# A four-layer graph network: four adjacency blocks built early, relation counts made turned

## What is computed

```
L0: key = x W_w + b; e = leaky_relu(s_dst[dst] + s_src[src]); alpha = softmax over dst
    x = LN(x + segment_sum(alpha * key[src], dst))
L1: x = LN(x + relu((x + segment_sum(x[src], dst)) @ W))
L2: messages silu(x[src] @ W + b) * edge weight, mean over dst, two-layer update, LN
L3: agg = segment_sum((x[src] + rel_emb[type]) @ W_msg.T + b_msg, dst) / degree; LN
```

## Time and profile before

| | |
|---|---|
| median of three runs | 1089.4 us (1089.07 to 1090.24) |
| the profiled execution | 1089.84 us, span 1088.0 us |
| PE busy | 1002.6 us, 92% of the span |
| PEld busy | 874.7 us, 80% |
| DVE busy | 861.1 us, 79% |
| ACT busy | 691.3 us, 64% |
| POOL busy | 218.2 us, 20% |

### The profile page before, as it was taken

The page is one execution under the profiler, slowest core; times in us unless marked ns, Lnnn a source line. Parts: engine busy times, 40 slices in busy tenths (PEclk is TensorE's granted clock), DMA queues, the critical chain, the costliest instruction groups (busy, mean ns, idle before and its releaser), DMA issues.

```text
span 1088.0 us, 27899 instructions
## 1 busy us (share of the span) xinstructions
PE 1002.6 (92%) x10463; PEld 874.7 (80%) x10463; DVE 861.1 (79%) x1934; ACT 691.3 (64%) x1489; POOL 218.2 (20%) x260
## 2 busy tenths in 40 slices
PE   3798979699999999995999999779999999989997
PEld 3343557599999999995788889669999999976775
DVE  6875999988998989987766677788787888766754
ACT  3467765454555555456888888577677776776554
POOL 4501340000000000000000000126666666610000
PEclk9899999899999999997999999889999999999998
DMA  6000020366767677752866564235444445334232
GB/s 159 1 2 1 4 68 3 121 207 225 238 215 225 222 238 227 204 175 72 292 195 193 172 201 141 82 104 140 138 136 129 131 131 139 109 112 124 69 99 82
DMA packets 86925, 150.38 MB, mean 138 GB/s; under 512 B 14524, under 2 KB 58375, under 8 KB 86557
## 3 DMA queue, kind: packets, MB, share of 16 engines
q1 hardware_dynamic: 65609, 116.01, 35.9%
q10 hardware_dynamic: 16122, 22.16, 5.7%
q0 software_dynamic: 5056, 10.36, 3.9%
HBM read 112.56 MB, written 35.94 MB: 136 GB/s over the span
## 4 chain that ended last, share of the span: by engine, by line
PE 81%; DVE 10%; ACT 4%; issue 3%; DMA 2%; POOL 0%; POOLq 0%; DVEq 0%; SPq 0%; ACTq 0%
PE PS L2500 14%; PE PS L2705 14%; PE PS L2488 11%; PE PS L2688 8%; PE PS L2611 7%; PE PS L2791 6%; PE PS L2581 3%; PE PS L2588 3%; PE PS L2326 2%; PE PS L2339 2%; DVE ring L1659 2%; DVE vo L1663 2%; PE PS L2403 2%; ACT X L1227 1%; PE PS L2357 1%
## 5 line engine op out<-in xcount | busy, mean ns | idle before, releaser
L1151 ACT CAST vo<-XT 128x768 f32<-128x768 bf16 (+1 forms) x218 | 180.3, 827 | 163.7 <-PE PS L2705 64.2
L984 POOL DMA_INDIRECT XT<-tab,ring x158 | 159.9, 1012 | 113.5 <-PE PS L2705 60.2
L2500 PE MATMUL PS<-vo 128*128 128x133 f32 x1300 | 175.9, 284 | 1.2 <-ACT vo L1151 1.2
L2500 PEld LDWEIGHTS PS<-vo 128*128 128x128 f32 x1300 | 157.2, 191 | 1.4 <-issue 1.4
L2488 PE MATMUL PS<-kp,ring 128*128 128x132 bf16 x1950 | 146.7, 221 | 3.2 <-DVE ring L1631 1.7
L2705 PE MATMUL PS<-vo 128*128 128x128 f32 x984 | 132.8, 279 | 0.0
L2488 PEld LDWEIGHTS PS<-kp,ring 128*128 128x128 bf16 x1950 | 125.6, 97 | 5.4 <-DVE ring L1631 1.8
L1641 DVE TENSOR_TENSOR XT<-iotab,XT 128x768 bf16<-128x768 bf16 (+1 forms) x218 | 120.0, 551 | 3.2 <-DMA hots_d<-XT 1.5
L2705 PEld LDWEIGHTS PS<-vo 128*128 128x128 f32 x984 | 118.9, 191 | 3.0 <-issue 2.4
L2490 PE MATMUL PS<-SDP,ring 128*128 128x12 bf16 x650 | 110.2, 170 | 0.0
L1286 ACT CAST adjf_r<-PS 128x512 fp32r<-128x512 f32 (+1 forms) x175 | 92.4, 550 | 25.4 <-PE PS L2581 23.6
(11 more groups left out here) (350 smaller groups left out, 2008.6 us busy)
## 6 DMA issues: line engine op xcount, KB each, us to landing
ring<-rows_d SPq DMA_DIRECT2D x146, 416.0 KB, 5.8
hots_d<-XT ACTq DMA_DIRECT2D x108, 192.0 KB, 4.7
big<-hots_d SPq DMA_DIRECT2D x10, 640.0 KB, 5.3
XT<-hots_d SPq DMA_DIRECT2D x10, 640.0 KB, 4.8
adj_d<-ring SPq DMA_DIRECT2D x20, 320.0 KB, 2.4
big<-hots_d SPq DMA_DIRECT2D x8, 480.0 KB, 4.4
adj_d<-ring SPq DMA_DIRECT2D x15, 240.0 KB, 2.1
ring<-adj_d SPq DMA_DIRECT2D x11, 320.0 KB, 3.0
```

The source lines that it names most:

```text
L984: G.indirect_dma_start(far_rows[:, f % FBUF, :], None, tab[2], bass.IndirectOffsetOnAxis(ap=far_row[:, t:t + 1], axis=0)).then_inc(far_in[ ...
L1151: C.copy(ohd[:, k % 3, 0:n, :], ohb[:, k % 3, 0:n, :]).then_inc(hots_wide, 1)
L2500: T.matmul(bank(6 + b % 2)[:, 0:VW], ohd[:, k % 3, i, :], vals[:, k % 3, i, :], start=j == 0, stop=j == JN - 1).then_inc(scattered, 1)
```

## The change

- `set_hots(0, NB)` and `set_hots(0, 0)` to `set_hots(0, 3)` move from the normalisation and layer one into layer zero's batches 103 to 106 on DVE. The copy of `SLc` that they need moves on ACT from behind layer zero into batch 101.
- SP loads the extras and chunks 0 and 1 as soon as the one-hots of the first four blocks are stored (18 batches). The wait for all stores moves ahead of chunks 2 and 3. These still stand behind `rc_cp` and the two DMAs of the reciprocal counts.
- PE builds steps 0 to 3 right after the last sum is copied, then transposes the reciprocal counts, then applies 0 and 1, builds 4 and 5, and so on.
- ACT widens steps 0 to 3 before the roots. Its byte copies of steps 0 and 2 stand behind `round_rows` 0 and 1 and behind `round_rows` 2. The last four rows (`ACT2`) are scaled one by one in steps 6 to 9, and `round_rows` 3, 4, 5 and 6 move to steps 5, 10, 12 and 14. DVE's `XL` 3 to 6 move to steps 6, 11, 13 and 15.
- The relation product has the 64 type columns as its stationary operand and moves the 128 columns of the destination one-hots. The result is turned already. `crelT`, its copy and `rel_turned` go; `rel_rows` reads bank 5 or 6 at step 2 of the next group. The product of zeros moves twice the columns and writes 64 partitions.
- The dense products wait for the last byte copy on ACT, for the last `sums_out1` from bank 3 on, and for `rel_rows` from bank 5 on.

```
+    EARLY_HOTS = HT * (NU - 1) // BT - 3
+    AHEAD = 4
+    LATE_ROWS = XBUF + 2
+    def rounded_at(i):
+        return XBUF + 1 if i < HBANK else LATE_ROWS + len(ACT2) + 2 * (i - HBANK)
 SP:
-                sp.wait_ge(hots_out[r], hots_stored(r))
+                sp.wait_ge(hots_out[r], 16 * len(range(r, (len(even(0)) * JN - 1) // BT + 1, 3)))
             extra_load(0); hots_load(0); hots_load(1)
...
                 if n == 0:
                     sp.wait_ge(hots_wide, NBATCH)
+                    for r in range(3):
+                        sp.wait_ge(hots_out[r], hots_stored(r))
                     hots_load(2)
 ACT:
+                if k == EARLY_HOTS - 2:
+                    C.copy(SLc[:, 1, :, :], SLc[:, 0, :, :]).then_inc(pairs_ready, 1)
...
+            for s in range(XBUF):
+                block_wide(s)
             for h in range(2):
                 deviations(1, h)
             act.wait_ge(scale_ready, 1)
             scaled_rows(X, range(0, QNB))
             for i in range(QBANK):
                 round_rows(1, i)
+            block_byte(0)
+            block_byte(1)
             scaled_rows(X, range(QNB, HNB - 4))
             for i in range(QBANK, HBANK - 1):
                 round_rows(1, i)
-            act.wait_ge(scale_ready, 2)
-            scaled_rows(X, ACT2)
+            block_byte(2)
+            block_byte(3)
             act.wait_ge(rc_tr, 1)
...
                     if s >= XBUF:
+                        block_wide(s)
+                        block_byte(s)
+                    if q == 0 and b == LATE_ROWS:
+                        act.wait_ge(scale_ready, 2)
+                    if q == 0 and 0 <= b - LATE_ROWS < len(ACT2):
+                        scaled_rows(X, [ACT2[b - LATE_ROWS]])
+                    for i in range(HBANK - 1, BANKS):
+                        if q == 0 and b == rounded_at(i):
+                            round_rows(1, i)
+                    if q and b == 2:
                         rel_rows(q - 1)
-                act.wait_ge(rel_mm, (q + 1) * NB)
-                C.copy(crelT[:, q % 2, 0:w // 2], bank(5 + q % 2)[:, 0:w // 2]).then_inc(crelT_cp, 1)
 DVE:
+                if k == EARLY_HOTS:
+                    dve.wait_ge(pairs_ready, 3)
+                    set_hots(0, NB, ohx[:, 0, :])
+                if 0 <= k - EARLY_HOTS < AHEAD:
+                    set_hots(0, k - EARLY_HOTS, ohs[:, k - EARLY_HOTS, :])
...
-                            if b == min(1 + i, NB - 1):
+                            if b == (1 + i if i < HBANK - 1 else rounded_at(i) + 1):
                                 dve.wait_ge(xp_top, i + 1)
 PE:
+                if s == 0:
+                    pe.wait_ge(vals_ready, NBATCH)
+                    pe.wait_ge(sums_cp, NB)
...
-                    o = T.matmul(bank(5 + q % 2)[:, d * NREL:(d + 1) * NREL], d1, r1, start=False, stop=False, skip_group_check=True)
+                    o = T.matmul(bank(5 + q % 2)[0:NREL, d * P:(d + 1) * P], r1, d1, start=False, stop=False, skip_group_check=True)
...
-            build(0)
-            build(1)
+            for s in range(XBUF):
+                build(s)
+            pe.wait_ge(cnt_ready, 1)
+            T.transpose(bank(4)[0:NB, 0:P], rc[:, :], ident[:, :]).then_inc(rc_tr, 1)
             for s in range(0, NS, 2):
                 for n in (s + 2, s + 3):
-                    if n < NS:
+                    if XBUF <= n < NS:
                         build(n)
                 for n in (s, s + 1):
                     if n < NS:
                         apply1(n)
-                        if n >= NB and n % NB == 7:
-                            rel_turned(n // NB - 1)
-            rel_turned(BANKS - 1)
...
             def sums1_wait(i):
                 pe.wait_ge(ag_ready, (even_need(i) if i < 3 else BANKS))
-                if i == 3:
+                if i == 5:
                     pe.wait_ge(crel_cp, BANKS)
-                if i >= 5:
-                    pe.wait_ge(crelT_cp, BANKS)
                 if i == 0:
+                    act_copied(pe, NS - 1)
                     pe.wait_ge(rc_cp, 1)
```

More of the change, by code:

```diff
@@ L1255, in round_rows, with block_wide, block_byte @@
                 C.copy(XH[:, nodes(i), :], X[:, nodes(i), :]).then_inc(xp_top, 1)
+            def block_wide(s):
+                w = even_width(s // NB)
+                act.wait_ge(adj_mm, s + 1)
+                if s >= XBUF:
+                    act.wait_ge(applied, s - XBUF + 1)
+                    dve_copied(act, s - XBUF)
+                C.copy(adjf[:, s % XBUF, 0:w], adj_bank(s)[:, 0:w]).then_inc(adjf_cp, 1)
+            def block_byte(s):
+                if not by_dve(s):
+                    adj_free(act, s)
+                    C.copy(adj_slot(s), adj_bank(s)[:, 0:even_width(s // NB)]).then_inc(adj_act, 1)
+            for s in range(XBUF):
+                block_wide(s)
             for h in range(2):
@@ L1651, in _, with set_hots @@
             FIRST = [h for h in units_at(0) if HT * h < 2 * BT]
+            def set_hots(q, j, buf):
+                V.tensor_tensor(buf.rearrange("p (k n b) -> p k n b", k=3, b=4), IN1[:, :, :].rearrange("p (k n) b -> p k n b", k=3),
+                                SLc[:, :, j, 4 * q:4 * q + 4].unsqueeze(2).to_broadcast([P, 3, NREL, 4]), ALU.is_equal).then_inc(ohs_ready, 1)
             dve.wait_ge(pool_consts, 8)
@@ L1923, in normalise @@
                     variance(1)
-                    set_hots(0, NB, ohx[:, 0, :])
                     scale(0)
@@ L1947, in split @@
                 low(BANKS - 1)
[L1949 to L1953, removed]
             normalise(1, X)
@@ L1985, in _ @@
                         sums_out1(q - 1)
-            for s in range(BANKS * NB - 4, BANKS * NB):
+            for s in range(BANKS * NB - AHEAD, BANKS * NB):
                 adj_copy(s)
@@ L2558, in build @@
                     if q >= 2:
-                        pe.wait_ge(crelT_cp, q - 1)
-                    T.matmul(bank(5 + q % 2)[:, 0:even_width(q) // 2], zeros[0:1, 0:P], zeros[0:1, 0:even_width(q) // 2],
+                        pe.wait_ge(crel_cp, q - 1)
+                    T.matmul(bank(5 + q % 2)[0:NREL, 0:even_width(q)], zeros[0:1, 0:NREL], zeros[0:1, 0:even_width(q)],
                              start=True, stop=False, skip_group_check=True)
                 pe.wait_ge(ohs_ready, q * JN + b + 2)
-                if s == 3:
-                    pe.wait_ge(rc_cp, 1)
+                if s == 0:
+                    pe.wait_ge(vals_ready, NBATCH)
+                    pe.wait_ge(sums_cp, NB)
                 if s >= 4:
@@ L2587, in build @@
                     _, d1, r1 = hots(*usual, d)
-                    o = T.matmul(bank(5 + q % 2)[:, d * NREL:(d + 1) * NREL], d1, r1, start=False, stop=False, skip_group_check=True)
+                    o = T.matmul(bank(5 + q % 2)[0:NREL, d * P:(d + 1) * P], r1, d1, start=False, stop=False, skip_group_check=True)
                     if b == 0:
                         _, d1, r1 = hots(*extra, d)
-                        o = T.matmul(bank(5 + q % 2)[:, d * NREL:(d + 1) * NREL], d1, r1, start=False, stop=False, skip_group_check=True)
+                        o = T.matmul(bank(5 + q % 2)[0:NREL, d * P:(d + 1) * P], r1, d1, start=False, stop=False, skip_group_check=True)
                 o.then_inc(rel_mm, 1)
-            def rel_turned(q):
-                pe.wait_ge(crelT_cp, q + 1)
-                pe.wait_ge(ag_ready, q + 1)
-                for d in range(len(even(q))):
-                    o = T.transpose(bank(3 + q % 2)[0:NREL, d * P:(d + 1) * P], crelT[:, q % 2, d * NREL:(d + 1) * NREL], ident[:, :])
-                o.then_inc(crel_tr, 1)
             def apply1(s):
@@ L2604, in apply1 @@
                 if b == 0 and q >= 2:
-                    pe.wait_ge(crel_cp, q - 1)
+                    pe.wait_ge(ag_ready, q - 1)
+                if b == 0 and q == 1:
+                    pe.wait_ge(rc_cp, 1)
                 if q == 0:
```

33 lines of the change are left out of this document (10 added, 23 removed).

## The result

The changed kernel takes 1133.24 us (median of 4 runs, 1132.64 to 1135.62), the kernel before 1089.82 us beside it (4 runs). The ratio is 1.0407, with a 95% interval of 1.0394 to 1.042: slower by 4%. The profiled execution took 1135.62 us with a span of 1133.8, against 1089.84 and 1088.0 before.

What follows compares the result with a forecast made beforehand. PE was taken as the limit, with 81% of the chain. +2.2 - 2.4 + 0.6 + 0 - 1.25 gave -0.85 us at the relu, taken as -0.7: median 1088.7 us, range 1085.5 to 1093.0.

Steps and rivals of the forecast that it cites:

- Part 6: Turned relation product, 650 on PE: bounds 0 to +4.5 us, -1.5 not excluded, taken as zero; narrow load held hidden.
- Rival 2: Turned product slower than before in each of 171 later builds: up to +4.5 us, 1093.2; chance 0.16.
- Rival 3: Load of 64 columns stands bare before each of 630 turned products, at least 0.05 us each: +31 us, 1120; chance 0.05.
- part 1: Early one-hots on DVE, loads on SP and copy on ACT in layer zero's late batches: cost zero.
- parts 1 and 2: Early one-hots, loads and copy cost zero; copy of the reciprocal counts (`rc_cp`) on ACT comes 1.0 us earlier.
- rival 4: PE starts late (501.4), table load delays the roots, `rc_cp` only 0.2 earlier: sum 0, 1089.5; chance 0.10.
- part 3: Blocks before chunk 2: build(10) starts at 523.9, PE idle 2 us; of about 3 us lead 1.0 is kept.
- Rings: ACT's round, DVE's `XL` and one-hots, PE's block at steps 10, 12, 14: 3.25, 3.25, 2.55 us; loss 3.2 us.
- part 4: Added wait three times in steps 10 to 16: loses 3.2 us, step 16 at 533.0, 2.2 us later than before.
- parts 5 and 7: Transposes gone from PE -2.4 us, larger product of zeros +0.6; dense products earlier at layer one's end -1.25.

Runs made afterwards that it cites:

- e5: Changed kernel with two neighbouring steps' adjacency products first, then their relation products, so half as many changes of width: 1112.97 us, ratio 1.0212.
- e1: Changed kernel with 128 loaded columns in the relation product (64 sources and 64 types) instead of 64: 1085.92 us, ratio 0.997.
- e7: Kernel before with only the relation product turned, at 128 loaded columns, in the old order of blocks: 1083.3 us, ratio 0.9946.
- e12: Changed kernel with 72 loaded columns in the relation product instead of 64: 1093.41 us, ratio 1.0032.
- e4: Changed kernel with 96 loaded columns in the relation product instead of 64: 1106.41 us, ratio 1.0145.
- e2: Changed kernel with the relation product, its copy and transposes as before, leaving the new order alone: 1092.24 us, ratio 1.0023.
- e9: e1 with DVE's subtractions of groups 3 to 6 two steps later, behind the one-hots PE waits for: 1084.03 us, ratio 0.9949.
- e8: Changed kernel with the 64 loaded columns' results in partitions 64 to 127 instead of 0 to 63: 1134.24 us, ratio 1.0403.

## Why the prediction was wrong

**Part 6 is the step that failed**, and it alone. It took the turned product at zero, with 0 to +4.5 us as bounds, "by the nearest row, the adjacency product beside it". That row has the moved side right and the loaded side wrong: it loads 128 columns, where the turned product loads 64. The one row with 64 loaded columns was the fp32 transpose, whose four follow each other and the apply without a gap, and from it I concluded that a narrow load is hidden. In those fp32 rows it is. In bf16, with the same 128x64 in the trace's rows, each change into it or out of it costs 0.135 us (e5), 4 changes to a pair. That makes 0.60 us for each pair against full width, and 0.57 against before. Fed with that, the prediction's own sum comes out: the 159 steps from step 16 on are some 80 pairs, by 0.57 45.6 us, less the 0.85 of the other parts 44.7, where 44.2 were measured. (The 0.57 is itself read in the kernel after; what this shows is that nothing else of size is missing.) The prediction's sign for a wrong product, pairs longer than 2.0 us, is what came.

**The rivals.** Rival 2 had the right place, each later build, with the wrong size and the wrong reason: moving 128 columns is cheaper than moving 64 (e1, e7). Rival 3 had the nearest time, 1120, and chance 0.05, but that is luck: bare loads of 0.05 for each product aren't it, since e5 has all the products and half the loss. What should have been weighed instead is a price per change of shape. The prediction says itself that "No row has this form", and a form without a row that stands 650 times on the bounding engine deserved wide bounds on the loaded side as on the moved one. The trace of before even holds a product of yet another shape, the product of zeros, which loads one row of 128 columns. Its chain at the opening of a group:

```profile
538.91 0.24 PE PS L2588 x4
539.15 0.21 PE PS L2560
539.36 0.35 PE PS L2581 x4
```

The adjacency product behind it takes 0.35 for four, 0.12 more than behind a relation product (0.23), and as long as behind the turned one of 64 columns. It is 0.35 in e1 too, where the zeros load 128 columns and move 512. With seven groups this weighs little in the sum, but it is a row in which an unchanged product takes longer behind one of another shape. Whether it is the same wait no run shows.

Two rules of the Trainium skill bear on it. The changed kernel and e5 show a wait at each change to 64 loaded columns, e12 and e4 none with 72 or 96. The Trainium skill (TensorEngine Tiling (Array Packing), sections Tiling Modes and Key Properties) lists 128x64 as a mode of its own and states that changing the mode drains the engine. The traces agree, at 0.135 us for one change; that the 64 columns run in that mode is inferred from this, no row of a trace names a mode. I hadn't weighed that rule. The rows of the loads show 145, 156 and 186 ns for 64, 72 and 96 columns and 113 for 128. The rule that I did weigh, fast weight load at the full 128 columns alone (the Trainium skill, TensorE: Matmul & The Clock Gate, section Weight-path perf modes — Fast Weight Load (FWL) and DoubleRow), agrees with that. The slower load costs about 0.007 us for each product of 64 columns (e5), 4 to 5 of the 47 us.

**Parts 1 to 5 and 7** can be read where 64 columns aren't in the way, in e2, on before's clock (+0.85):

- The early one-hots cost nothing (part 1): e2's sum copies lie 0.84 earlier than before's from the first on, and its last one 0.85.
- First apply: predicted 510.5, measured 510.44. The first block's product in the kernel after: 500.4 and 500.33. Build(4) starts at 514.12 and build(7) at 518.60, where 514.2 and 518.6 were predicted.
- Copy of the counts: 513.3 and 513.25, 1.1 before the old one (parts 1 and 2 hold). In the kernel after it was 513.59: its four early blocks hold the changes of width too, so ACT's table load ends 506.78 - 1.46 = 505.32, and the root begins 0.5 late. A table load that ends after 505.2 was the sign of rival 4, and its mechanism is there, at less than half its size (0.34 of the 0.8 us), but not from its cause: PE started on time, at 500.33, and its blocks were longer.
- Build(10): 523.9 and 523.82, with PE idle for 1.61 us, ended by the DMA of chunk 2; 2 were predicted (part 3). In the kernel after PE is idle for only 0.38 there, since its blocks take longer.
- Rings: 3.25, 3.25, 2.55 predicted, 3.27, 3.29, 2.58 measured; step 16 at 533.0 predicted, 532.96 measured (part 4). e9 shows the cause by taking it away. The loss of 2.2 us is 2.3 at the relu of e2.
- Transposes -2.4, zeros +0.6, end -1.25 (parts 5 and 7): together -3.05. e7 has -5.0 at the relu. The rest, -2.0, fits the product itself at 0.22 instead of 0.24 for four: pairs of 1.91 instead of 1.94, 80 times, are -2.4. Part 6 had -1.5 as its bound below zero; it had read 0.22 for four old ones from one place of a timeline, and the chain has 0.24. The product of zeros is 0.11 longer on the chain (0.32 against 0.21), as taken. In the kernel after it is 1.25 us from the start of the last group product (727.59) to the relu; 1.2 was predicted.

So apart from the 64 loaded columns the change is a small gain: +2.3 - 5.0 = -2.7 at the relu by its halves, -2.9 in e1, with a median of 1085.92 against 1090.33 before.

## What to carry to other kernels

Before a product is turned, look at what becomes its loaded side: 64 columns in place of 128 make another shape of product, and on this kernel each change between the two (0.135 us) costs more than two products (0.056 us each). Where such products alternate with full ones, fill the loaded side to 128 with columns that lie beside it, even if their results are thrown away. And where the nearest row differs from the new form on one side, bound that side by itself; a row of another type (fp32 transposes here) is no row for it. A wait that is moved on one engine is paid for by what stands behind it in that engine's order: e9 moved four such instructions by two steps and got 3.4 us back.

## What the runs showed of the hardware

- A bf16 product with 64 loaded columns among products with 128: 0.135 us for each change of width, into it and out of it (e5), also out of it into fp32 products of full width (the apply, 1.14 instead of 0.98). Which half the 64 columns stand in doesn't matter (e8: 1134.24 against 1133.24). With 72 and 96 loaded columns a change costs nothing: adjacency and apply behind them take 0.22 and 0.98 to 0.99, as in e1. Widths under 64 weren't run.
- The bf16 loads below full width that were run are slower than full ones: medians 145, 156, 186 ns for 64, 72, 96 columns and 113 for 128, and products of 128 moved columns follow each other at 0.061, 0.068, 0.089 and 0.056 us.
- With 128 loaded columns, moving 128 takes 0.056 us a product, and moving 64, as before did with a stride, 0.060. Moving fewer columns doesn't pay here; what the stride has to do with it isn't shown.
- Left open: why the fp32 transposes with 64 loaded columns (load 111 ns) cost nothing at their changes. No run varied their type. The Trainium skill (TensorEngine Tiling (Array Packing), section Restrictions) states that column tiling and fp32 transposes exclude each other. That would fit; no run here shows it.
